# Layer 1's attention: queries and keys ahead of the values, key sums behind, and five small steps in other periods

## The reference, cut to what matters

```python
Q = jax.nn.relu(x @ Wq + bq)
K = jax.nn.relu(x @ Wk + bk)
V = jax.nn.relu(x @ Wv + bv)
scores = jnp.einsum('bqhd,bkhd->bhqk', Qh, Kh) / np.sqrt(dh)
key_mask = jnp.sign(jnp.abs(jnp.sum(x, axis=-1)))
scores = jnp.where(key_mask[:, None, None, :] == 0, NEG, scores)
scores = jnp.where(tril[None, None, :, :] == 0, NEG, scores)
attn = jax.nn.softmax(scores, axis=-1) * query_mask[:, None, :, None]
out = jnp.einsum('bhqk,bkhd->bqhd', attn, Vh).reshape(B, T, U) + x
# then layer norm with gamma, beta, and the residual
```

## Time and profile before

| | us |
|---|---|
| median of 3 runs | 1055.17 (1055.07 to 1057.11) |
| the profiled execution | 1055.3 |
| its span, first to last instruction | 1054.0 |
| busy: TensorE 988.4, VectorE 871.8, ScalarE 778.3, GpSimd 452.3 | |
| layer 1's attention, first to last score products | 735.1 to 949.2 |

### The profile page before, as it was taken

How to read it: one execution, slowest core, us unless ns; L and a number is a source line. 1 busy time by engine, 2 the same in 40 slices (tenths; PEclk the granted TensorE clock), 3 DMA queues, 4 the chain that set the end, 5 groups by cost and what they waited for, 6 DMA issues and landing times.

```text
span 1054.0 us, 25523 instructions
## 1 busy us (share of the span) xinstructions
PE 988.4 (94%) x8777; PEld 779.7 (74%) x8777; DVE 871.8 (83%) x3717; ACT 778.3 (74%) x2132; POOL 452.3 (43%) x531
## 2 busy tenths in 40 slices
PE   5999999999999999889979999999889999999887
PEld 5898878888888888643248988888667777776556
DVE  5776878787878888779998899888878888896995
ACT  5876767676777767648787888776678888887766
POOL 1434535362635353505900012101878888893001
PEclk9999999999999999999999999999999999999899
DMA  9000000000000000000000000000000000000002
GB/s 396 2 2 2 2 2 2 1 2 1 2 2 2 2 2 2 2 0 1 1 1 1 1 1 2 1 11 11 22 22 21 22 23 22 22 2 2 1 2 81
DMA packets 8578, 18.36 MB, mean 17 GB/s; under 512 B 1280, under 2 KB 5504, under 8 KB 8064
## 3 DMA queue, kind: packets, MB, share of 16 engines
q1 hardware_dynamic: 8448, 16.72, 4.7%
HBM read 10.42 MB, written 2.10 MB: 12 GB/s over the span
## 4 chain that ended last, share of the span: by engine, by line
PE 70%; DVE 15%; ACT 9%; issue 3%; POOL 2%; DMA 1%; ACTq 0%; SPq 0%; DVEq 0%; POOLq 0%
PE PB L239 6%; PE PB L241 6%; PE PB L240 6%; PE PB L389 5%; PE PB L405 5%; PE PB L372 5%; PE PB L334 4%; PE PB L1568 4%; ACT W L353 3%; PE PB L1056 3%; PE PB L1058 3%; PE PB L1057 3%; PE PB L1540 3%; PE PB L1585 3%; PE PB L424 2%
## 5 line engine op out<-in xcount | busy, mean ns | idle before, releaser
L353 ACT ACTIVATE W<-W,small 128x128 f32<-128x128 f32 x512 | 198.7, 391 | 118.2 <-DVE small L344 85.1
L364 POOL TENSOR_TENSOR W<-W,small 128x512 f32<-128x512 f32 x128 | 133.6, 1044 | 241.9 <-DVE small L358 241.9
L239 PE MATMUL PB<-RR_s 128*128 128x256 f32 (+3 forms) x544 | 176.3, 324 | 4.9 <-DVE RR_s L1008 2.5
L241 PE MATMUL PB<-RR_s 128*128 128x256 f32 (+3 forms) x544 | 167.4, 308 | 0.0
L240 PE MATMUL PB<-RR_s 128*128 128x256 f32 (+3 forms) x544 | 167.3, 308 | 0.0
L1556 POOL TENSOR_TENSOR AR_s<-AR_s,small 128x512 f32<-128x512 f32 x128 | 129.4, 1041 | 31.9 <-DVE small L1549 31.8
L1030 ACT ACTIVATE AR_s<-PB,W 128x512 f32<-128x512 f32 (+2 forms) x160 | 100.6, 630 | 28.9 <-PE PB L241 22.4
L344 DVE CUSTOM_DVE_ANT_0 W<-PB,W 128x128 f32<-128x128 f32 x512 | 113.4, 285 | 2.8 <-PE PB L334 0.3
L239 PEld LDWEIGHTS PB<-RR_s 128*128 128x128 f32 x544 | 104.1, 191 | 14.5 <-issue 4.7
L1549 DVE CUSTOM_DVE_ANT_0 AR_s<-PB,W 128x128 f32<-128x128 f32 x512 | 111.4, 286 | 3.7 <-PE PB L1540 0.9
L1044 DVE TENSOR_TENSOR RR_s<-AR_s,RR_s 128x512 fp32r<-128x512 f32 (+2 forms) x160 | 99.8, 633 | 17.3 <-ACT RR_s L1035 14.1
(11 more groups left out here) (356 smaller groups left out, 2328.5 us busy)
## 6 DMA issues: line engine op xcount, KB each, us to landing
W<-in_w SPq DMA_DIRECT2D x1, 5873.0 KB, 24.1
XF<-in_xT SPq DMA_DIRECT2D x4, 512.0 KB, 9.3
out<-XT SPq DMA_DIRECT2D x8, 256.0 KB, 2.3
W<-in_w SPq DMA_DIRECT2D x1, 1088.0 KB, 5.3
W<-in_w SPq DMA_DIRECT2D x1, 1024.0 KB, 8.2
W<-AR_s SPq DMA_DIRECT2D x16, 64.0 KB, 2.1
AR_s<-AR_s SPq DMA_DIRECT2D x16, 64.0 KB, 2.1
QS<-AR_s SPq DMA_DIRECT2D x12, 64.0 KB, 2.1
```

Of the source, the lines that this page charges most:

```text
L239: nc.tensor.matmul(out, lh, rh, start=True, stop=False)
L241: return nc.tensor.matmul(out, lh, rl, start=False, stop=True)
L353: e = nc.scalar.activation(SS[r][:, hl], SS[r][:, hl], ACTF.Exp, bias=mx[r][:, h:h + 1], scale=-1.0, accum_out=rc[r][:, h:h + 1])
L364: nc.gpsimd.tensor_tensor(s3, s3, over(rc[r], 2, [128, 4, 128]), ALU.mult).then_inc(s_nrm, 1)
```

## The change

It alters only the order of work. In each period TensorE has a new place, "projected", between PV and the values, for query and key; the key sums become a step of their own at s = 16c+7, behind the values. The two counts on s_kp change places, in the expert stage too. Query 1 goes from s = 2 (period 0) to s = 6 (period 1, just ahead of key 1), and with it TensorE's wait for the expert stage's last output goes from period 0 to period 1, behind the score products. VectorE's masks of chunk 0 go from between the maxima of period 1 to behind them. The third factor step goes from s = 15 (period 3) to s = 18 (period 4). The slot mean becomes a VectorE step of its own at s = 22 (period 5), one period ahead of its product.

```diff
--- before.py
+++ after.py
@@ -1202,12 +1202,12 @@
         def act_key(c, out, KT):
             if c:
                 act.wait_ge(s_kd[(c - 1) % 2], spreads(c - 1))
-            act.wait_ge(s_kp, 2 * c + 2)
+            act.wait_ge(s_kp, 2 * c + 1)
             nc.scalar.activation(KT, out[:, :], ACTF.Relu, bias=w("bk")).then_inc(s_kt, 1)
 
         def dve_key(c, sums, KT):
 
-            dve.wait_ge(s_kp, 2 * c + 1)
+            dve.wait_ge(s_kp, 2 * c + 2)
             dve.wait_ge(s_kt, c + 1)
             nc.vector.scalar_tensor_tensor(KT, sums[:, :], 0.0, KT, ALU.not_equal, ALU.mult).then_inc(s_kx, 1)
 
@@ -1251,9 +1251,9 @@
                         pe.wait_ge(s_gt, 28)
                         pe_query(0, PB[6])
                     if AHEAD.get((n, k)) == 1:
-                        pe_keysum(0, PB[7])
                         pe.wait_ge(s_qt, 1)
                         pe_key(0, PB[6])
+                        pe_keysum(0, PB[7])
                     if n < NJ:
                         pe_up(n, k)
                     if n and 4 * n + k < 4 * NJ + 3:
@@ -1431,10 +1431,14 @@
         def aside(s):
 
             c, i = divmod(s, 16)
-            if c < 7 and i in PROJECT:
+            if s == 6:
+                yield "query", 1
+            if c < 7 and i in PROJECT and s != 2:
                 yield PROJECT[i], c + 1
-            if s in (10, 14, 15):
-                yield "factors", (10, 14, 15).index(s)
+            if s in (10, 14, 18):
+                yield "factors", (10, 14, 18).index(s)
+            if s == 22:
+                yield "mean", 0
             if s == 26:
                 yield "b1", 0
             for i, what in FINISH.items():
@@ -1453,8 +1457,9 @@
             if what == "query":
                 passes5(("q", c), 4, s_qt, c + 1)
             if what == "key":
+                passes5(("k", c), 4, s_kt, c + 1)
+            if what == "keysum":
                 passes5(("ks", c), 6, s_kx, c + 1)
-                passes5(("k", c), 4, s_kt, c + 1)
             if what == "tokens":
                 passes5(("x", c), 6, s_xc, c + 1)
             if what == "b1":
@@ -1474,7 +1479,7 @@
                     if what in kinds:
                         plan_aside(what, c)
 
-        TURNED, MULTIPLIED = ("tokens", "gamma"), ("query", "key", "factors", "b1", "select", "add")
+        TURNED, PROJECTED, MULTIPLIED = ("tokens", "gamma"), ("query", "key"), ("keysum", "factors", "b1", "select", "add")
 
         NB5 = U // 4
 
@@ -1491,6 +1496,7 @@
                 plan_asides(q, TURNED)
                 if q >= 2:
                     passes5(("o", q - 2), 4, s_o5, q - 1)
+                plan_asides(q, PROJECTED)
                 if q + 1 < NB5:
                     passes5(("v", q + 1), 6, s_vt, q + 2)
                 plan_asides(q, MULTIPLIED)
@@ -1657,10 +1663,12 @@
             act_query(c, bank5(("q", c)), QT)
 
         def pe_key5(c):
+            pe_drained5(("k", c))
+            pe_key(c, bank5(("k", c)))
+
+        def pe_keysum5(c):
             pe_drained5(("ks", c))
             pe_keysum(c, bank5(("ks", c)))
-            pe_drained5(("k", c))
-            pe_key(c, bank5(("k", c)))
 
         def act_key5(c):
             act_key(c, bank5(("k", c)), KT)
@@ -1733,10 +1741,12 @@
                 mm = nc.tensor.matmul(bank5("b1")[64 * k:64 * k + 64, 0:1], w("fw1b"), smean, start=True, stop=True)
             mm.then_inc(s_b1m, 1)
 
-        def dve_b1(i):
+        def dve_mean(i):
             nc.vector.tensor_reduce(smean, w("slotT"), AX.X, ALU.add).then_inc(s_b1, 1)
             dve.wait_ge(s_b1, 1)
             nc.vector.tensor_scalar(smean, smean, 1.0 / 64, None, ALU.mult).then_inc(s_b1, 1)
+
+        def dve_b1(i):
             dve.wait_ge(s_b1m, 1)
             nc.vector.tensor_tensor(b1e, bank5("b1")[:, 0:1], w("fb1"), ALU.add).then_inc(s_b1, 1)
 
@@ -2331,22 +2341,24 @@
             pe_tokens5(0)
             pe_v5(0)
             turned = {"tokens": pe_tokens5, "gamma": pe_gamma5}
-            multiplied = {"query": pe_query5, "key": pe_key5, "factors": pe_factors, "b1": pe_b1, "select": pe_select5, "add": pe_add5}
+            projected = {"query": pe_query5, "key": pe_key5}
+            multiplied = {"keysum": pe_keysum5, "factors": pe_factors, "b1": pe_b1, "select": pe_select5, "add": pe_add5}
             for q in range(NB5):
                 if q:
                     pe_S5(q)
                 if q == 4:
                     pe.wait_ge(s_pa, added(NJ - 1))
+                if q == 1:
+                    pe.wait_ge(s_ty, NJ)
                 if q:
                     pe_T5(4 * q - 4)
                     pe_T5(4 * q - 3)
                 steps_of(turned, q)
                 if q >= 2:
                     pe_PV5(q - 2)
+                steps_of(projected, q)
                 if q + 1 < NB5:
                     pe_v5(q + 1)
-                if q == 0:
-                    pe.wait_ge(s_ty, NJ)
                 steps_of(multiplied, q)
                 if q:
                     pe_T5(4 * q - 2)
@@ -2424,7 +2436,7 @@
             dve_add(NJ - 1)
             dve.wait_ge(s_pa, added(NJ - 1))
             dve_v5(0)
-            beside = {"keysum": dve_keysum5, "masks": dve_masks5, "factors": dve_factors, "b1": dve_b1,
+            beside = {"keysum": dve_keysum5, "masks": dve_masks5, "factors": dve_factors, "mean": dve_mean, "b1": dve_b1,
                       "gamma": dve_gamma5, "select": dve_select5, "add": dve_add5}
             for q in range(NB5):
                 if q >= 3:
@@ -2432,12 +2444,12 @@
                 if q:
                     dve_max5(4 * q)
                     dve_max5(4 * q + 1)
-                if q == 1:
-                    dve_masks5(0)
                 step_of(beside, 4 * q)
                 if q:
                     dve_max5(4 * q + 2)
                     dve_max5(4 * q + 3)
+                if q == 1:
+                    dve_masks5(0)
                 step_of(beside, 4 * q + 1)
                 if q + 1 < NB5:
                     dve_v5(q + 1)
```

## The result

The changed kernel takes 1046.35 us (median of 4 executions, 1046.02 to 1048.74), the kernel before 1055.12 in the same job (4 executions, 1054.34 to 1057.11). The ratio is 0.9917, with a 95% interval of 0.9904 to 0.9931: 8.8 us less, between 7.3 and 10.1. The forecast was 1046.6.

What follows compares the result with a forecast made beforehand. TensorE's order of work was taken as the bound. Opening and period 4 2.2, key of period 5 0.62, mean 1.1, five chunks 4.75: 8.7 off 1055.3 gives 1046.6; own range 1045.2 to 1048.2, 8-in-10 range 1043.3 to 1050.3.

Steps and rivals of the forecast that it cites:

- Key periods: Periods q = 5, 9, ..., 25: the whole stop before the late transposes goes, 6 x 0.62 = 3.7 us.
- Query periods: Periods q = 4, 8, ..., 24: query 0.33 earlier, gaining 0.33 in five, 1.6 us; all 0.62 in q = 4.
- Relu 1.12 behind it: Query periods: ScalarE's Relu follows the moved query product by 1.12 us, at 769.37, with the bank free at 770.10.
- The opening: Periods 0 to 3: query 1, masks and third factor moved; period 4 starts 3.5 early and ends 2.2 early.
- The new wait: Query and key wait for the copy of the transpose before them; costed at nothing, 0.6 a period if exposed.
- The mean: Periods 6 and 7: the 1.72 stop goes, GpSimd's root gives part back; 12.82 instead of 13.94, net 1.1.
- A: Rival: GpSimd binds the steady periods, so the steady gains (4.75) go; 1051.3 us, chance 0.08.
- C: Rival, slower: GpSimd binds with its handshakes in series, 27.74 a chunk against 27.57; 1056.3 us, chance 0.03.
- ScalarE's wait for GpSimd's subtract: Sign against the forecast: it is wrong if ScalarE waits for GpSimd's subtract longer than before the change.
- D: Rival: the transpose waits for the o5 copy in the other bank, query and key gain nothing; 1052.6, chance 0.05.
- B: Rival: last stage's clock changes; half-clock dip (at most 3.4 us) vanishes, 1043.2, chance 0.08, or second dip, 1050.0, chance 0.10.

Runs made afterwards that it cites:

- late applies: The changed kernel with ScalarE's four applies one step later, behind the o5 copy: 1050.79 us, ratio 0.9957 to the kernel before.
- loaded kernel: The changed kernel with one more GpSimd instruction of about 1.04 us in each of periods 8 to 27: 1051.06 us, ratio 0.9958 to the kernel before.
- ahead only: The kernel before with only queries and keys ahead of the values, key sums behind, query 1 still in period 0: 1052.38 us, ratio 0.9962.
- factor only: The kernel before with only the third factor step moved from period 3 to period 4: 1054.90 us, ratio 0.9985.

## Why the prediction was right

Where each period starts, against the first score products, and how much earlier that is than before:

| step | forecast | measured |
|---|---|---|
| S5(1), query 1 gone from period 0 | 1.71 | 1.72 |
| S5(2) | 0.95 | 0.93 |
| S5(3), masks behind the maxima | 1.4 | 1.25 |
| S5(4), third factor gone | 3.5 | 3.49 |
| S5(5), factor and query of period 4 | 2.2 | 2.32 |
| S5(6), key of period 5 | 2.85 | 2.95 |
| periods 6 and 7 | 12.82, 1.1 less | 12.81, 1.13 less |
| five settled chunks | 4.75 (0.95 each) | 4.21 (0.85 each) |
| sum | 8.7 | 8.29 |

**Key periods.** Right in full: 6.99 to 7.00 and no idle time before the transposes. Here the sums and values both stand between the key and the transposes, 2.05 us from 774.38 to 776.43, enough for product, Relu and handshake.

**Query periods.** The term that was mis-sized, and that the sum shows: 0.33 forecast, 0.23 measured, in five of them. The chunks are 0.54 short by it, and as the start of period 6 and the mean's periods came 0.13 better than forecast, the sum is off by 0.4. The step that failed is "Relu 1.12 behind it". That distance was read where the product stood behind the values or the sums. Directly behind PV, ScalarE's Relu comes 1.22 to 1.23 later, of query and key alike: 794.21 to 795.43, and 774.38 to 775.61. ScalarE's timeline after:

```profile
775.61 0.69 ACT L1206 ACTIVATE AR_s<-PB,W 128x512 f32<-128x512 f32 x1 [0.22 <-PE PB L1200]
...
795.43 0.69 ACT L1194 ACTIVATE AR_s<-PB,W 128x512 f32<-128x512 f32 x1 [0.24 <-PE PB L1188]
```

It waited for the product both times, so the o5 copy, at nothing in the forecast, wasn't the cause. In key periods the margin took up the tenth, in query periods there was none. The product itself takes 1.13 directly behind PV (794.21) and 1.02 behind the values. A row at hand had said so of another such place: 1.12, for the query behind a stop. The tenth belongs to the place, not to the query: the values product is recorded with 0.49 where it stands first behind PV (768.25 in the earlier trace rows) and with 0.38 behind the query or key (795.17, 775.35). So of the 0.33 that the values stood ahead of the query 0.11 were the cost of standing first, and the query took that cost over; values and query together take 1.19 (768.25 to 769.44) before and 1.18 (794.21 to 795.39) after. Why the first product behind PV costs more stays open; nothing was run for it.

**The opening.** Its end, S5(4), is right by two errors that cancel. The second of the masks' instructions (L1694) takes 1.01 at 748.27, where it took 0.67 before (L1686), GpSimd's value work waits 0.34 for the masks (749.60), and period 3 starts 1.25 earlier and not 1.4. Why that instruction is longer there stays open. Period 3 then loses 2.24 and not the 2.1 that the forecast had taken off it.

**The new wait** of query and key for the copy two passes before: costed at nothing. No row in the steady periods shows one. In period 1, where no PV stands between, query 1 waits 0.53 for it (744.39), and nothing comes later for that: S5(2) was 0.93 earlier, as forecast.

**The mean.** Right in its size, and by an order of work that was half right. The forecast let ScalarE's applies start with GpSimd's root and everything queue behind them. The late applies showed that GpSimd's subtract, queued behind the same root, arrives late by itself. Both hang on the root, so the number came out the same.

**The rivals.** A and C, GpSimd as the bound: it binds period 7, as the forecast had it, but in the steady chunks it has about 3.2 us to spare, and C's sum of busy time and waits is the reckoning that the loaded kernel refuted. ScalarE's wait for GpSimd's subtract, a sign that the forecast named, is 0.55 in the steady periods before and after; only in period 1 it is longer, 1.46 at 746.29. D: the transposes did follow the Relu, and the key stop was gone. B: the last stage kept its stretch of half clock and its length, 99.05; the clock moved ahead of the stage instead, where two executions of one kernel differ by 2.5 (736.80 and 734.29). A forecast from one profiled execution carries that. Nor is B's price of 3.4 for such a stretch borne out. Where the changed kernel's second execution has a granted clock of 0.50 and 0.50 in two stretches of 3.40 us (976.50 to 983.30), the kernel with the third factor in period 7 has 0.86 and 0.64 in the same part (974.82 to 981.62), and its last stage takes 99.04 against 99.06. In all four kernels of which the trace has only some 3.5 us of low clock there (GpSimd loaded, third factor in period 7, applies later, query ahead of PV) it takes 98.65 to 99.04, so the other half of the stretch cost 0.4 at most. TensorE only waits longer for VectorE there; its timeline in the one and in the other:

```profile
978.79 1.11 PE L2089 MATMUL PB<-W,AR_s 128*128 128x128 f32 x4 [0.39 <-DVE AR_s L2014]
```

```profile
977.12 1.04 PE L2089 MATMUL PB<-W,AR_s 128*128 128x128 f32 x4 [1.19 <-DVE AR_s L2014]
```

**The clock and the median.** The stage gave 8.29 and the medians lie 8.77 apart, within the interval; the 0.5 between could be clock. So it is partly luck that the median came within 0.3 of the forecast: the stage itself gave 0.4 less than the forecast's 8.7. Of kernels that keep the stops of 1.7 to 2.8 us in periods 0 and 6, one or both of them, two of six traces (ahead only, factor only) show half clock behind both, at 0.9 (7.17 against 6.26) and 1.5 (15.49 against 13.94) in the first; the other four show none in this stage. The changed kernel has neither stop. That this is worth 0.5 on the median isn't shown.

## What to carry to other kernels

Where engines pass tiles through a short ring of banks, look for the pass whose reader is the last to finish before the next one wants its bank, and put other products of the same engine between the two: the order alone took 0.62 out of each key period. Measure the reader's distance where the product will stand, not where it stands now, and ask whether a neighbour's time belongs to the neighbour or to its place: the first product behind PV cost a tenth more, whichever it was. A stop that is left (period 7's 1.64) is a free place: ask which engine makes it before moving that engine's work, and put the first engine's spare work there.

## What the runs showed of the hardware

A stop of TensorE lowered its clock in one execution and not in another. Behind the same stop of 1.93, four 128x256 products took 2.08 us once and 1.13 once, and 32 score products took 2.09 behind a stop of 2.81, at a granted clock of 0.51. The stretches with a granted clock near a half lie, in the two executions of one kernel, at 455 to 461.5 and 980.5 to 987.5 in one, at 533 to 536, 546.5 to 550 and 976.5 to 983.5 in the other. The Trainium skill, TensorE: Matmul & The Clock Gate, section "What's actually happening", says that the monitor's window runs freely and that the same kernel therefore varies from run to run. These rows agree that one kernel varies; whether the window is the reason no run here shows.

A stretch of low clock need not cost time. In period 1 it cost 0.9 of a period of 6.26, in periods 6 and 7 1.5 of 13.94. In the last stage half of such a stretch was gone with no change of the stage's length (99.06 and 99.04).

A part of a change can so look like a loss in one trace (221.24 against 219.84) where the periods that it touches are 1.08 shorter. Cutting the trace by period, and reading the clock of each, is what told the two apart.
